# A graph-attention kernel on one Trainium2 core: the neighbour rows of the last quarter are fetched in sets of eight lanes, and its sums lie in PSUM banks of their own

## What is computed

```
h   = relu(layernorm(x))
Wh  = h @ W
e   = leaky_relu(Wh @ a[:128] (by row) + Wh @ a[128:] (by column), 0.2)
e   = where((adj > 0) | eye, e, -9e15)
x   = x + softmax(e, axis=1) @ Wh
x   = x + where(adj < 1, exp(-2 (1/adj - 1)^2), 0) @ (relu(layernorm(x)) @ W1 + B1)
```

## Time and profile before

| | |
|---|---|
| median of 3 runs | 222.34 us (221.56 to 222.77) |
| profiled execution | 221.81 us, its span 219.9 us |
| busy: ACT / DVE / PE / POOL | 187.4 / 182.9 / 159.4 / 134.6 us |
| loads of `adj` | 32 of 2 MB, median 22.3 us from issue to landing |
| indirect DMAs | 48 for own words, 28 for shared words |
| mean granted clock of TensorE | 0.89 |

### The profile page before, as it was taken

The page is one execution under the profiler, slowest core; times in us unless marked ns, Lnnn a source line. Parts: engine busy times, 40 slices in busy tenths (PEclk is TensorE's granted clock), DMA queues, the critical chain, the costliest instruction groups (busy, mean ns, idle before and its releaser), DMA issues.

```text
span 219.9 us, 3227 instructions
## 1 busy us (share of the span) xinstructions
PE 159.4 (72%) x957; PEld 110.3 (50%) x970; DVE 182.9 (83%) x543; ACT 187.4 (85%) x199; POOL 134.6 (61%) x134
## 2 busy tenths in 40 slices
PE   0188779971944992989929995995759749956971
PEld 0077555430532761558625762673526417645971
DVE  7993999999569999999489979784895999398853
ACT  0699986799999999998999959999999969999400
POOL 3970000593000588988777888797577888587740
PEclk9999999997699698599985999699696996996796
DMA  6999999999999999999999999999999999811302
GB/s 165 356 414 410 408 411 406 411 413 416 420 412 406 408 396 402 392 399 397 399 388 384 399 396 399 393 390 399 388 394 389 400 396 404 327 45 22 107 12 101
DMA packets 22388, 76.83 MB, mean 349 GB/s; under 512 B 2643, under 2 KB 3255, under 8 KB 22368
## 3 DMA queue, kind: packets, MB, share of 16 engines
q1 hardware_dynamic: 18912, 71.31, 83.0%
q0 software_dynamic: 3040, 5.22, 7.0%
q10 hardware_dynamic: 416, 0.07, 0.2%
HBM read 74.40 MB, written 4.23 MB: 358 GB/s over the span
## 4 chain that ended last, share of the span: by engine, by line
issue 24%; DVE 22%; PE 21%; ACT 12%; POOL 12%; DMA 7%; POOLq 0%; DVEq 0%; ACTq 0%
POOL gathered_rows L507 7%; PE bank L613 7%; DVE summed L1074 6%; DMA hub_whe<-node_table 5%; ACT spread L879 5%; PE bank L724 4%; POOL gathered_rows L476 3%; DVE hub_w L1334 3%; PE bank L709 2%; DVE cand L1112 2%; ACT trash_a L910 2%; ACT gathered_rows L885 2%; PE bank L716 2%; ACT whe L893 1%; DMA gathered_rows<-node_table,shared_index 1%
## 5 line engine op out<-in xcount | busy, mean ns | idle before, releaser
L507 POOL DMA_INDIRECT gathered_rows<-node_table,index x48 | 73.8, 1538 | 39.2 <-issue 36.1
L613 PE MATMUL bank<-adj_ring,pack_w 128*128 128x512 bf16 (+3 forms) x259 | 73.0, 411 | 4.0 <-DMA adj_ring<-in_adj 2.9
L910 ACT ACTIVATE trash_a<-adj_ring,below_one 128x4096 fp8e4<-128x4096 f32 x19 | 70.4, 3705 | 3.4 <-DMA adj_ring<-in_adj 2.8
L915 ACT ACTIVATE trash_a<-adj_ring 128x4096 fp8e4<-128x4096 f32 x19 | 68.7, 3617 | 0.6
L1074 DVE SCALAR_TENSOR_TENSOR summed<-adj_ring 128x4096 fp8e4<-128x4096 f32 x13 | 57.6, 4431 | 1.5 <-DMA adj_ring<-in_adj 1.4
L613 PEld LDWEIGHTS bank<-adj_ring,pack_w 128*128 128x128 bf16 x262 | 26.8, 106 | 34.6 <-issue 11.0
L507 POOL DMA_INDIRECT gathered_rows<-node_table,shared_index x28 | 37.8, 1351 | 8.5 <-issue 7.9
L1112 DVE MAX8 cand<-bank 128x8 f32<-128x120 f32 (+25 forms) x82 | 23.3, 349 | 3.5 <-PE bank L613 3.4
L724 PE MATMUL bank<-gathered_rows,spread 128*128 128x129 f32 x176 | 22.4, 283 | 1.5 <-DVE spread L1317 1.5
L724 PEld LDWEIGHTS bank<-gathered_rows,spread 128*128 128x128 f32 x176 | 21.3, 197 | 1.9 <-issue 1.7
L600 PE MATMUL bank<-codes,code_w 128*128 128x512 bf16 x22 | 10.0, 456 | 10.2 <-DVE adj_ring L1090 6.2
(11 more groups left out here) (169 smaller groups left out, 259.8 us busy)
## 6 DMA issues: line engine op xcount, KB each, us to landing
adj_ring<-in_adj SPq DMA_DIRECT2D x32, 2048.0 KB, 22.3
node_table<-gathered_rows POOLq DMA_DIRECT2D x4, 520.0 KB, 8.3
x_sb<-in_x SPq DMA_DIRECT2D x8, 256.0 KB, 5.8
out<-x_sb SPq DMA_DIRECT2D x3, 512.0 KB, 14.7
gathered_rows<-node_table,index POOLq DMA_INDIRECT x48, 5.7
gathered_rows<-node_table,shared_index POOLq DMA_INDIRECT x28, 5.5
out<-x_sb SPq DMA_DIRECT2D x2, 192.0 KB, 1.9
out<-x_sb SPq DMA_DIRECT2D x1, 128.0 KB, 1.9
```

Source lines behind the costliest of these rows:

```text
L507: pool.indirect_dma_start(out=rows[:, g % RING_GROUPS * GE + t, :], out_offset=None, in_=table, in_offset=bass.IndirectOffsetOnAxis(ap=row ...
L613: last = nc.tensor.matmul(to[:, lo:hi], pack_w[:, k, :], ring_hi[:, i % AR, row_at + lo:row_at + hi], start=False, stop=(k == KB - 1), ski ...
L910: nc.scalar.activation(trash_a[:, :], ring[:, i % AR, :], ACT.Sign, bias=below_one[:, :], scale=-1.0, accum_out=signs[:, n:n + 1], saturat ...
L915: nc.scalar.activation(trash_a[:, :], ring[:, i % AR, :], ACT.Abs, accum_out=sizes[:, n:n + 1], saturate=False).then_inc(checked_a, 1)
```

## The change

The shared words of piece 3 aren't fetched on their own any more. The best 16 of each set of eight lanes are handed on and are merged with those of step 15, and both are fetched with the last four DMAs. So the last quarter has 8 + 4 indirect DMAs instead of 8 + 4 + 4, and the groups are 0 to 9: group 9 is the last one. To this belong new masks and a score table for sets of eight (`own_oct`, `kc_of_m`, `oct_of_m`, `same_oct`, `s_by_oct`, `oct_scores`, `r_oct`), four rounds of `pick_shared(4)` over 80 words on 16 partitions instead of two over 32 on 32, and wider weights in `weigh_last`.

The sums of the last quarter lie in banks 0 to 2, those of the words, so that `add_columns(3)` waits for the scans of steps 14 and 15 and not for `epilogue(2)`. The work at the end is ordered anew: `weigh` is cut into `edge_weights` and `spread_weights`; the verdicts (`judge_early`) move from DVE to POOL, behind its DMAs; `decode_shared(4)` stands ahead of `epilogue(2)`. In the loop `add_columns(2)` moves from chunk 29 to 28, `add_own(2)` from 30 to 29, `scatter(6)` from 31 to 30, and `place(3)` stands behind `add_own(2)`. `hub_whe` is copied from SBUF, ahead of the table's stores, and not read back from memory.

```diff
-PIECES = [..., ((12, 13, 14), 16, 8, 16), ((15,), 8, 0, 16)]
+PIECES = [..., ((12, 13, 14), 16, 8, 0, 8), ((15,), 8, 0, 32, 8)]
+HANDED, LEFT = 3, 16
...
-SCATTER_AT = {14: 0, 17: 1, 19: 2, 22: 3, 26: 4, 27: 5, 31: 6}
+SCATTER_AT = {14: 0, 17: 1, 19: 2, 22: 3, 26: 4, 27: 5, 30: 6}
...
-ADD_COLUMNS_AT = {13: 0, 21: 1, 29: 2}
+ADD_COLUMNS_AT = {13: 0, 21: 1, 28: 2}
...
-ADD_OWN_AT = {13: 0, 21: 1, 30: 2}
+ADD_OWN_AT = {13: 0, 21: 1, 29: 2}
...
+        def acc_bank(s, n):
+            return bank[n if s == SG - 1 else 4 + n]
...
+            pool.dma_start(hub_whe[:, :], scaled[0:P // KB, 0:KB, :]).then_inc(hub_whe_loaded, 16)
...
-            pool.wait_ge(first_stored, 16)
-            pool.dma_start(hub_whe[:, :], table[0:P, :]).then_inc(hub_whe_loaded, 16)
...
-                else:
+                elif s < SG - 1:
                     pe.wait_ge(acc_read, s)
                 weights = col_weights(s)
                 for t in range(KB):
+                    if s == SG - 1 and t in (0, 6):
+                        pe.wait_ge(scanned, 2 * (STEPS - 1) + t // 6)
...
+            add_columns(SG - 1)
             place(4)
+            place_shared(4)
             scatter(7)
-            place_shared(4)
-            add_columns(SG - 1)
             add_own(SG - 1)
             scatter(8)
-            scatter(9)
...
+                merge_to = oct_words[:, LEFT:LEFT + w] if n == HANDED + 1 else shared_cand[0:sets, 0:w]
+                words = oct_words[:, 0:LEFT + w] if n == HANDED + 1 else merge_to
+                best_of = oct_words if n == HANDED else shared_slots[0:sets, :]
...
-            decode_shared(3)
+            edge_weights(7)
             scan(STEPS - 1)
             pick(4)
+            spread_weights(7)
             pick_shared(4)
-            judge_early()
+            decode_shared(4)
             epilogue(2)
-            decode_shared(4)
             weigh(8)
-            weigh(9)
             weigh_last(0)
```

More of the change, by code:

```diff
@@ L93 @@
 MAX_LANE = max(LANE_SLOTS)
-MAX_SLOTS = max(slots for _, slots, _, _ in PIECES)
+MAX_SLOTS = max(slots for _, slots, _, _, _ in PIECES)
+OL = 8
 MERGE_COL, SHARED_COL = 64, 192
@@ L665, in place @@
                 pe.wait_ge(shared_set, 7)
-                for q in range(HK):
+                pe.wait_ge(oct_set, 4)
+                own, sets = (own_oct, LANES) if SET_LANES[n] == OL else (own_lane, 32)
+                for q in range(SET_LANES[n]):
                     at = MERGE_COL + q * REST[n]
-                    last = nc.tensor.matmul(to[0:32, at:at + REST[n]], own_lane[:, q, :],
+                    last = nc.tensor.matmul(to[0:sets, at:at + REST[n]], own[:, q, :],
                                             slots[:, LANE_SLOTS[n]:LANE_SLOTS[n] + REST[n]],
@@ L708, in add_columns @@
                 for t in range(KB):
-                    last = nc.tensor.matmul(acc_of(t), weights[:, t, :], hub_whe[:, GQ:GQ + E1], start=(t % 3 == 0),
+                    if s == SG - 1 and t in (0, 6):
+                        pe.wait_ge(scanned, 2 * (STEPS - 1) + t // 6)
+                    last = nc.tensor.matmul(acc_of(s, t), weights[:, t, :], hub_whe[:, GQ:GQ + E1], start=(t % 3 == 0),
                                             stop=True, skip_group_check=True)
@@ L753, in spread_hub @@
                 for t in range(KB):
-                    last = nc.tensor.matmul(acc_of(t)[0:P // KB, :], where[:, t, :], hub_rows, start=False,
+                    last = nc.tensor.matmul(acc_of(0, t)[0:P // KB, :], where[:, t, :], hub_rows, start=False,
                                             stop=True, skip_group_check=True)
@@ L1147, in pick_shared @@
             def pick_shared(n):
-                w, rounds = HK * REST[n], SHARED_ROUNDS[n]
+                lanes, rounds = SET_LANES[n], SHARED_ROUNDS[n]
+                w, sets = lanes * REST[n], P // lanes
+                before = sum(SHARED_ROUNDS[:n])
                 source = bank[4] if n == 0 else bank[7]
+                merge_to = oct_words[:, LEFT:LEFT + w] if n == HANDED + 1 else shared_cand[0:sets, 0:w]
+                words = oct_words[:, 0:LEFT + w] if n == HANDED + 1 else merge_to
@@ L1179, in pick_shared @@
+                nc.vector.tensor_scalar(full[0:sets, n, 2:3], best_of[:, end - 1:end], 1.0 / lanes, None,
                                         ALU.mult).then_inc(shared_seen, 1)
             def decode_shared(n):
-                w = TURNS[n]
+                o, w, lanes = SHARES.index(n), TURNS[n], SET_LANES[n]
                 source = (bank[4] if n == 0 else bank[7])[:, SHARED_COL:SHARED_COL + w]
+                mask_of = oct_mask if lanes == OL else shared_mask
+                lane_on = lane_is_mem[:, 0:w * lanes].rearrange("p (e q) -> p e q", q=lanes)
@@ L1247, in weigh, with edge_weights @@
             def weigh(g):
+                edge_weights(g)
+                spread_weights(g)
+            def edge_weights(g):
                 n, s = PIECE_OF_GROUP[g], SUPER_OF_GROUP[g]
```

363 lines of the change are left out of this document (203 added, 160 removed).

## The result

| | before | changed |
|---|---|---|
| median | 222.23 us (219.35 to 223.46, 20 runs) | 220.62 us (218.94 to 222.78, 20 runs) |
| ratio to before | | 0.9946 [0.9923, 0.997] |
| profiled execution | 221.81 us, span 219.9 us | 221.1 us, span 219.3 us |
| mean granted clock of TensorE | 0.89 | 0.90 |

The kernel got faster, by some 1.2 us (0.54%) by the ratio, 1.6 us by the medians. The forecast was 2.8 us. The sign and the range (217.8 to 221.8) held; the size didn't: by the ratio it is less than half of what was predicted.

A forecast was written before the change was run, and what follows sets the result against it. Behind the stream, TensorE's chain waiting for `epilogue(2)` was taken as the bound, GpSimd 1.4 us behind. The summed steps moved VectorE's last addition from 216.39 to 213.6, 2.8 us off the 222.34 median: 219.5 us, range 217.8 to 221.8.

The forecast's parts named there:

- the earlier `scan(15)`: Behind the stream on VectorE: the scan starts at 193.50, right behind `edge_weights(7)`, not at 195.82, 2.3 us earlier.
- the way from the four rounds to `epilogue(2)`: Rounds end at 199.1, `place_shared(4)` takes 0.4 us, `scatter(7)` 3.0 from 199.5, so `epilogue(2)` begins at 202.5.
- GpSimd is 1.4 us behind the bound: At the end of the kernel before: last gathered rows are there at about 212.5, `weigh_last(3)` takes them at 213.91.
- the 1.4 us that I gave to own banks alone: Own banks without fewer DMAs would run into GpSimd after 1.4 us of gain.
- Early parts, `hub_whe`, chunks 28 to 31: New masks, tables, the `hub_whe` copy and moved loop steps cost nothing, since the stream of `adj` covers them.
- the rival "slower": In chunks 28 to 31, a late `epilogue(1)` holds up `pack(29)` and what follows: 224 us if 5.5 us late; chance 0.08.
- A start after 192: Sign against the prediction: `pack(31)`, forecast at 191.5 or 0.3 us later, starting after 192.
- if group 7's rows land at another time: Sign against the prediction: the gathered rows of group 7 not landing at 192.58 as before.
- nothing gained: Rival: `epilogue(2)` waits for `scatter(7)`, `place_shared(4)` and the rounds; rounds at 1.1 us leave 0.8 gained, 221.6 us; chance 0.09.
- Mixed: TensorE's clock between 199 and 211 us is partly full, partly half; otherwise the prediction is wrong.
- both of the clock's rivals: TensorE's clock full: 4.8 us gained, 217.5 us, chance 0.16; half throughout: 0.8 us gained, 221.5 us, chance 0.17.
- a constant 3.5 us: From VectorE's last addition to the end of the span: 3.5 us of last store and flag, which stay.

The follow-up runs named there:

- b1: The kernel before with own banks for the last quarter's sums alone, `add_columns(3)` ahead of `place(4)`: 222.32 us, ratio 0.9981.
- b5: The kernel before with own banks for the last quarter's sums alone, `add_columns(3)` left behind `place_shared(4)`: 221.67 us, ratio 0.997.
- u4: The changed kernel with banks 4 to 6 for all quarters and TensorE's order of before: 222.47 us, ratio 1.0023.
- b0: The kernel before, unaltered, run again for a second trace: 221.73 us, one execution.
- b4: The kernel before, unaltered, run again for a fourth trace: 222.48 us, one execution.
- u2: The changed kernel with `hub_whe` read back from the table in memory, behind all its stores: 220.95 us, ratio 0.994.
- c1: The changed kernel, unaltered, run again for a third trace: 220.56 us, one execution.
- c0: The changed kernel, unaltered, run again for a second trace: 220.59 us, ratio 0.9914.
- e2: The changed kernel with `scatter(7)` ahead of `place_shared(4)` on TensorE: 219.2 us, ratio 0.9853.
- e3: The changed kernel with `weigh(8)` ahead of `epilogue(2)` on VectorE: 218.48 us, ratio 0.9799.
- e4: The changed kernel with `scatter(7)` ahead of `place_shared(4)` and `weigh(8)` ahead of `epilogue(2)`: 217.11 us, ratio 0.9766.
- e1: The changed kernel with 14 unused products on TensorE between `place(4)` and `place_shared(4)`: 220.19 us, ratio 0.9893.
- b6: The kernel of b5 with `decode_shared(4)` and `weigh(8)` ahead of `epilogue(2)`, the verdicts behind it, all 16 DMAs kept: 222.95 us, ratio 1.0014.
- b3: The kernel before, unaltered, run again for a third trace: 222.5 us, one execution.

## Why the prediction was right in sign and wrong in size

**The step that failed.** The mechanism was right and two terms of the sum were mis-sized: the earlier `scan(15)`, which the sum took at 2.3 us with "the rows of group 7 land at 192.58 as before" and which is 1.1 us by the mean of four traces, and the way from the four rounds to `epilogue(2)`, where `scatter(7)` took 3.81 us in two of three traces in place of 3.0. The next parts take them one by one.

**What bounds the kernel.** Right in the main. TensorE's chain and GpSimd are both near the end in the kernel before, and neither half alone gains: b1 and b5 give 0.9981 and 0.997, u4 1.0023, the changed kernel 0.9946. That GpSimd is 1.4 us behind the bound holds for the one trace: in b0 and b4 VectorE waits over 2 us for gathered rows. Of the 1.4 us that I gave to own banks alone b5 shows some 0.7, and its interval reaches just beyond no gain; the rest goes into a new wait and the clock.

**Early parts, `hub_whe`, chunks 28 to 31.** Right at nothing. u2 shows it for `hub_whe`. `add_columns(2)` took 2.02 us from 179.22, `pack(29)` began at 181.67 and `pack(31)` at 192.06, with an idle wait for its chunk just ahead: the rival "slower" had no ground. A start after 192 was to be a sign against the prediction, and two of three traces of the changed kernel have one (192.06, 192.44); but two of four of the kernel before do too, and the means are the same, 192.0.

**The scan 2.3 us earlier.** This is the first term that was mis-sized. In the changed kernel the scan stands 2.0 us behind `pack(31)`, as forecast (193.5 - 191.53), but by luck: the forecast had it set by `edge_weights(7)` ending at 193.50, and in the trace these are done at 191.02 and the scan waits for `pack(31)`. Where it stood in the kernel before was wrong: 4.29 us in the one trace that I had, 3.10 in the mean of four. I wrote that the prediction would be wrong "if group 7's rows land at another time"; they do, by 1.7 us between executions of the same kernel. It is not only the scan: the whole stretch from `pack(31)` to the last addition is 24.86 us in the earlier trace rows and 23.95 in the mean. That takes 0.9 us off the 2.8. The time of that execution gave no warning, since an earlier `pack(31)` (0.5 us) and a shorter tail (0.8 us) than the mean hid the longer stretch in it.

**From the four rounds to `epilogue(2)`.** Forecast 199.1 for their end, 7.6 us behind `pack(31)`; measured 199.79, 7.7. A round takes 0.59 (I took 0.6), so the price on which "nothing gained" hung falls. `place_shared(4)` took 0.58 and not 0.4, being at half the clock. `scatter(7)` I gave 3.0 us from 199.5; it took 3.81 from 200.35 in the first trace and 3.81 in c1, and 3.01 in c0, where the clock fell halfway through. `epilogue(2)` began at 12.1 us behind `pack(31)`, forecast 11.0. So 1.2 us are lost here in two of three traces. The price for half the clock was a misreading as well: the 3.42 us in the earlier trace rows that I took for it ended at 206.62, and by the earlier trace rows the clock was full again from 206.1 on. Wholly at half, 16 products take 3.8 us.

**The clock.** One fall, brought by the first gap, as I had it, but its place varies: 1.6 us after the idle stretch began in the first trace (196.45 to 198.1), 2.8 in c1, 4.6 in c0, where the earlier trace rows had given about 4. That is the whole spread between `scatter(7)` at 3.81 and at 3.01 us. There was no second fall: the last turns ran at the full level (28 products in 3.36 us behind an idle stretch of 2.01). From `epilogue(2)` to `finish_last(0)` it took 7.1 us in place of 7.6: 0.5 us back. "Mixed" was right, both of the clock's rivals fall. Behind it all `finish_last(0)` began 19.3 us behind `pack(31)` (forecast 18.6), and the mean distance of the last addition is 22.45 us, against 22.07 in the sum. On this side the sum missed by 0.4 us; with the 0.9 of the other side that is the 1.3 us between the 2.8 of the forecast and the 1.5 of the traces (1.6 by the medians).

**The gaps.** In the earlier trace rows a gap of 2.33 us was followed by a fall of the clock. In the changed kernel the gap was 3.39 us and the clock fell, in the first trace when the gap was 1.6 us old. In e2 a gap of 3.48 us ahead of 205.42 had no fall behind it while work went on (the last products there took 3.37 us for 28). The Trainium skill (TensorE: Matmul & The Clock Gate, Why this matters for your kernels) would let gaps of up to about 3 us pass. The changed kernel's whole gap agrees with that, the other two don't. The length of one gap alone didn't decide here, and the measurements stand.

**The size of the missed gain.** The prediction put `epilogue(2)` ahead of `weigh(8)` and `scatter(7)` behind `place_shared(4)` into its sum, as the change has them, and priced neither order. e2, e3 and e4 do: 1.4, 2.1 and together 3.5 us. The rival "nothing gained" named exactly this chain (`epilogue(2)` for `scatter(7)` for `place_shared(4)` for the rounds), and looked for its price in the rounds, where it wasn't.

**What stays open.** From the last addition to the end of the span I took a constant 3.5 us. It is 3.4 to 5.2 in the traces without a relation to the edits. In it the DMA queues show only the last stores and a few packets of instructions. A part is the landing of the last store, 1.9 us in every trace of before, but 3.0 and 2.9 in the changed kernel's first trace and c1 and 4.7 in e1; b0 and b4 have 4.8 and 5.0 us behind the last addition with a store of 1.9 us, so it isn't all. What decides the rest wasn't found.

## What to carry to other kernels

Before a wait is priced from one trace, ask what it waits for and whether that moves from run to run: a stretch measured from the last fixed event, in three or four executions of the same kernel, would have given 1.1 us for 2.3. When a change frees one engine, walk through the order of the others once more: here a product whose inputs were there stood behind one whose inputs were 3.4 us away, and an epilogue that nobody waited for stood ahead of weights that TensorE waited for. One line moved in each of two queues was worth 3.5 us, over twice the change itself, and VectorE's part of it brought nothing in the kernel with all 16 DMAs (b6 against b5).

## What the runs showed of the hardware that I hadn't expected

- An indirect DMA mostly takes GpSimd 0.99 to 1.00 us to issue, and 5.01 us where it lies beside VectorE's check of a chunk (4.42 us long): 179.26 to 184.27 in the changed kernel.
- 16 products of 128x129 on the gathered rows take 1.95 to 2.05 us at the full clock and 3.65 to 3.81 where all or nearly all of them ran at half.
- In the kernel before, own banks left TensorE idle for 1.92 us ahead of 44 products, and these took 6.79 us, against 5.08 in b3, where `add_columns(3)` and `add_own(3)` ran right ahead of them. The clock was at its lower level for 3.4 us in both, in b3 under those two (203.8 to 207.2), in b5 under the 44 products (206.9 to 210.3): the fall moved with the wait.
